# Attention stage of a gated cross-attention and expert kernel: the next group's front product issued before or after the probability-value products

## The reference

```python
x = x + tanh(g_xattn) * attention(layernorm(x), ctx, ctx, mask, Wq, bq, Wk, bk, Wv, bv)
    # Qh, Kh, Vh = 16 heads of 16; probs = softmax(masked(Qh Kh^T / sqrt(10))); probs @ Vh
x = x + tanh(g_ffn) * experts(layernorm(x), Wg, W1, W2, W3)
    # per expert: top-k tokens; silu(xg W1^T) * (xg W3^T) @ W2^T, weighted, added back
```

## Time and profile before

| | |
|---|---|
| median of 3 runs | 1004.09 us (1002.74 to 1007.72) |
| profiled execution, its own time | 999.87 us |
| its span, first to last instruction | 998.1 us |
| mean granted TensorE clock | 0.913 of full speed |
| busy: PE, PEld | 783.9 us (79%), 615.0 us (62%) |
| busy: DVE, ACT, POOL | 608.9 us (61%), 516.7 us (52%), 401.4 us (40%) |
| 256 score maxima, L684 | 165.0 us, 676 ns each |
| 256 exponentials, L541 | 147.6 us, 587 ns each |
| 2048 values matmuls, L852 | 72.1 us |

### The profile page before, as it was taken

How to read it: one execution, slowest core, us unless ns; L and a number is a source line. 1 busy time by engine, 2 the same in 40 slices (tenths; PEclk the granted TensorE clock), 3 DMA queues, 4 the chain that set the end, 5 groups by cost and what they waited for, 6 DMA issues and landing times. The chain is left out here.

```text
span 998.1 us, 22875 instructions
## 1 busy us (share of the span) xinstructions
PE 783.9 (79%) x7244; PEld 615.0 (62%) x7244; DVE 608.9 (61%) x1501; ACT 516.7 (52%) x1002; POOL 401.4 (40%) x777
## 2 busy tenths in 40 slices
PE   3488888798889888987897721116899999999994
PEld 1366666566666665665666511112798899889884
DVE  1457777677667667766767618879545544644530
ACT  2356576657665666666566711000555665666551
POOL 3344334433443344334432132003355675575434
PEclk9799999999999899989999955555899999999997
DMA  3875558656866585667556235001154365453223
GB/s 116 233 202 129 162 173 237 172 167 178 227 156 180 159 220 148 186 185 184 155 144 159 71 94 186 0 1 44 44 109 119 72 128 113 109 92 47 55 33 42
DMA packets 99261, 130.60 MB, mean 131 GB/s; under 512 B 12896, under 2 KB 62336, under 8 KB 99200
## 3 DMA queue, kind: packets, MB, share of 16 engines
q1 hardware_dynamic: 86912, 112.78, 40.2%
q0 software_dynamic: 12288, 17.05, 10.5%
HBM read 52.34 MB, written 26.49 MB: 79 GB/s over the span
## 5 line engine op out<-in xcount | busy, mean ns | idle before, releaser
L684 DVE TENSOR_REDUCE m_sb<-a_ps 128x4 f32<-128x512 f32 x256 | 165.0, 676 | 17.5 <-PE a_ps L825 16.4
L541 ACT ACTIVATE p_t<-b_ps 128x512 f32<-128x512 f32 x256 | 147.6, 587 | 52.4 <-PE b_ps L838 50.3
L1351 POOL DMA_INDIRECT out<-y,idx_add x64 | 100.1, 1565 | 107.8 <-DVE idx_add L1451 71.6
L825 PE MATMUL a_ps<-k_st,q_st 97*128 97x128 bf16 x1024 | 100.2, 221 | 21.7 <-DMA k_st<-k_part 16.2
L1341 POOL DMA_INDIRECT xg<-rows_scratch,idx x64 | 67.7, 1058 | 103.6 <-issue 89.1
L455 POOL TENSOR_TENSOR q_part<-q_rest,q_part 128x512 bf16<-128x512 f32 x32 | 36.9, 1154 | 179.4 <-ACT q_part L512 179.4
L825 PEld LDWEIGHTS a_ps<-k_st,q_st 97*128 97x128 bf16 x1024 | 73.9, 98 | 55.4 <-issue 48.9
L838 PE MATMUL b_ps<-q_st,k_st 99*128 99x128 bf16 x1024 | 100.2, 221 | 4.7 <-ACT p_t L541 4.7
L1549 PE MATMUL bank<-x_hi,w_hi 128*128 128x512 f32 x256 | 100.7, 393 | 1.5 <-DVE x_lo L1477 1.5
L1549 PE MATMUL bank<-x_hi,w_lo 128*128 128x512 f32 x256 | 99.9, 390 | 0.0
L1549 PE MATMUL bank<-x_lo,w_hi 128*128 128x512 f32 x256 | 99.7, 390 | 0.0
(11 more groups left out here) (193 smaller groups left out, 1728.4 us busy)
## 6 DMA issues: line engine op xcount, KB each, us to landing
q_st<-q_part SPq DMA_DIRECT2D x96, 256.0 KB, 4.7
k_st<-k_part SPq DMA_DIRECT2D x96, 256.0 KB, 4.1
w<-in_w_t SPq DMA_DIRECT2D x24, 512.0 KB, 4.9
rows_scratch<-row SPq DMA_DIRECT2D x16, 528.0 KB, 4.1
x_in<-in_x SPq DMA_DIRECT2D x16, 512.0 KB, 4.9
c_t<-in_ctx_t SPq DMA_DIRECT2D x16, 512.0 KB, 4.9
x_res<-in_x SPq DMA_DIRECT2D x16, 512.0 KB, 3.7
out<-x SPq DMA_DIRECT2D x16, 512.0 KB, 3.3
```

The costliest lines, as they stand in the source:

```text
L541: act.activation(p_t[b.s % 2][:, 4 * q:4 * q + 4, :], b_ps[q % 2][:].rearrange("p (h s) -> p h s", s=P), ACT.Exp, scale=SCALE).then_inc(ex ...
L684: dve.tensor_reduce(m_sb[b.s % 2][:, 4 * q:4 * q + 4], a_ps[q % 2][:].rearrange("p (h s) -> p h s", s=P), AX_X, ALU.max).then_inc(max_done, 1)
L825: mm = pe.matmul(a_ps[q % 2][:, i * P:(i + 1) * P], q_st[g.p][0:A_K, h, tok], k_st[g.p][0:A_K, h, tok], start=True, stop=True)
L1351: pool.indirect_dma_start(out[:, :], bass.IndirectOffsetOnAxis(ap=idx_add[e.p][:, st:st + 1], axis=0), y[st][:], None, compute_op=ALU.add) ...
```

## The change

In quarter 2 of each step the front product of the next group is issued before `values`, `router` and `scores_back` instead of behind them. Quarter 0 does the same as before.

```diff
                     if q == OT_AT:
                         out_back(b)
                     scores_t_(*((b.back(2), q - 1) if q else (b.back(3), 3)))
+                    if q in (0, 2):
+                        front(g.on(1), 2 * b.j + q // 2)
                     if q == 2:
                         for i in range(4):
                             values(b.back(3), i)
...
                         if b.j == 1:
                             scores_back(g.on(-3), b)
-                    if q in (0, 2):
-                        front(g.on(1), 2 * b.j + q // 2)
                     if q == 0:
                         max_t(b)
```

## The result

The changed kernel takes 1012.62 us (median of 18 runs, 1008.32 to 1018.13), the kernel before in the same sittings 1004.68 us (18 runs, 1001.71 to 1008.53). The ratio is 1.0077, with a 95% interval of 1.006 to 1.0093: slower by 7.9 us, where +7.5 us was forecast and 1011.6 us named. The sum came out; its two terms did not, as the traces show: that the total is so near is luck. The profiled executions stand further apart, with spans of 998.1 and 1010.6 us. Of these 12.5 us, 7.3 are there at the last `router_out` (593.19 us after, 585.90 before). The other 5.2 come behind it, where the two programs are the same: that stretch took 412.2 us in the trace of before, 417.4 in that of after and 414.3 to 417.5 in those of the experiments. So the loss that belongs to the change is the one in the attention, and it is near the 7.9 us of the medians.

A forecast was written before the change was run, and what follows sets the result against it. The prediction took a closed chain through GpSimd's `ln1` and `rest_k` to bound the kernel, not TensorE's own work. Delay +4.2 us and clock falls +3.3 us gave +7.5 us on 1004.1, 1011.6 us, range 1003.5 to 1019.

The forecast's parts named there:

- its two terms: The forecast's +4.2 us for a delay in groups 1 to 14 and +3.3 us for more clock falls.
- What bounds the kernel: Claim that a chain through GpSimd, not TensorE's own work, sets the group spacing, 33.36 us in the loop.
- The circle through `split_q`, `ln1`, `rest_k` and `mid_k`: Closed chain from k_st through TensorE, GpSimd and ScalarE back to k_st; its delay reaches the group nearly one for one.
- The forecast's own sign against it: The forecast called itself wrong if groups kept 33.36 us despite the new wait; then the circle would be another.
- The new wait for `rest_q`: Step j = 1: the moved front product u = 3 waits 0.44 us on TensorE for the first half's `rest_q`.
- I take 0.30 us per group: Delay of the third quarter's exp, `mid_q`, `split_q` and `ln1`; over 14 groups +4.2 us.
- 2.0 us idle before L908: TensorE's idle time waiting there for late ScalarE (L561) was to grow from 1.5 to about 2.0 us.
- One or two more clock falls, +3.3 us: Loop groups in which longer TensorE idle time lowers the granted clock, at 2.6 us each, beyond the three before.
- the piece that looked like a small win: Shorter wait before u = 4, 0.83 to about 0.6 us, bringing TensorE about 0.23 us sooner to L908.
- Faster: Rival: u = 3 sooner by 1.18 us speeds `hi_q`, `rest_q`, `mid_q` and GpSimd's start; -16.5 us, 987.6; chance 0.06.
- Nothing: Rival: `rest_q` is in time or slack absorbs the stall; 1004, down to 1001.7 us; chance 0.13.
- clock falls widely: Rival: four to five more clock falls in the loop besides the delay; +16 us, 1020; chance 0.14.

The follow-up runs named there:

- e7: Kernel before, with `ln1` on GpSimd ahead of the two `split_q` in step j = 1 instead of behind them: 973.99 us, ratio 0.9679.
- e4: Kernel before, with 12 extra identity matmuls on TensorE in each group before its wait at L908: 1004.28 us, ratio 0.9982.
- e3: Changed kernel, with 12 extra identity matmuls on TensorE in each group before its wait at L908: 1004.65 us, ratio 0.9988.
- e12: Kernel before, order untouched, with one memset of an unused tile on GpSimd at the start of `ln1`: 1019.09 us, ratio 1.0129.
- e9: Changed kernel, with 6 extra matmuls of 256 columns per group before the wait at L908, in the loop only: 1000.57 us, ratio 0.9948.
- e2: Kernel before, with the front products of steps j = 0, 2 and 3 moved ahead but not that of j = 1: 1005.47 us, ratio 1.0002.
- e6: Kernel before, with 12 extra identity matmuls per group before the wait at L908, in the loop only: 1037.45 us.
- e10: Kernel before, with 6 extra matmuls of 256 columns per group before the wait at L908, in the loop only: 1016.59 us.

## Why the prediction was right in its sum and wrong in its split

*What bounds the kernel: right.* The circle through `split_q`, `ln1`, `rest_k` and `mid_k` held: opening it (e7) gave 3.2%. The forecast's own sign against it, groups that keep 33.36 us despite the new wait, came all the same (33.39). What was wrong is not the circle but how much of the delay reaches `rest_k`.

*The new wait for `rest_q`: right in place, 0.55 us of delay instead of 0.44.* 0.37 us of it are the later start behind the transposed scores (the idle time in the row of L804 is 0.29), 0.18 are seams, where the forecast allowed for some hundredths.

*"I take 0.30 us per group", +4.2 us: wrong, about three times too large.* The spacing grew by 0.03 and 0.18 us in the two groups that can be compared and by 0.10 between e4 and e3, an estimated 1.4 us in all. `mid_q` did slip by 0.38 us, but `rest_k`, at the other end of `ln1`, by less: from the first `rest_q` to this row

```profile
329.14 1.16 POOL L460 TENSOR_TENSOR k_rest<-k_val,k_part 128x512 f32<-128x512 f32 x1 [0.18 <-POOL nm L435]
```

it is 329.14 - 315.48 = 13.66 us, and 392.61 - 379.09 = 13.52 before. Where the other 0.24 us went, two rows of the trace of before show:

```profile
390.32 0.48 DVE L717 SCALAR_TENSOR_TENSOR x<-o_n,gx,x_res 128x256 f32<-128x256 f32 x1
390.39 0.47 POOL L427 TENSOR_TENSOR t<-t,v 128x4 f32<-128x4 f32 x1 [0.18 <-POOL t L426]
```

GpSimd's two-input instruction started inside VectorE's `finish` and took 0.47 us instead of the 0.20 us of its like. In the changed kernel the 0.38 us put another instruction of the chain there, later in that of VectorE, and it got off with 0.22 us:

```profile
326.47 0.49 DVE L717 SCALAR_TENSOR_TENSOR x<-o_n,gx,x_res 128x256 f32<-128x256 f32 x1
...
326.79 0.22 POOL L426 TENSOR_TENSOR t<-y 128x4 f32<-128x4 f32 x1 [0.18 <-POOL y L429]
```

So the two engines got out of each other's way by 0.25 us, and most of the shift was swallowed. It is so in every loop group: before, one instruction of each `ln1` took 0.47 or 0.34 us, in turn, and none did in the changed kernel; from `rest_q` to `rest_k` it is 13.52 or 13.44 us before and 13.66 or 13.62 after. The delay that arrives is 0.14 or 0.18 us. (The Trainium skill, "SBUF — State Buffer", summary of rules, says that of a VectorE and a GpSimd instruction the second one waits fully for the first when VectorE reads two inputs from SBUF and the GpSimd instruction reads SBUF. The rows agree: 390.39 + 0.47 ends within 0.06 us of 390.32 + 0.48.) The step that failed was to carry a delay through a chain of 16 instructions of another engine as if their durations did not depend on when they run. In e12 too 0.52 us put in became 0.35 us of spacing; where the rest of it went was not traced.

*"2.0 us idle before L908": right (1.89 to 1.94), and right in its reason.* It is TensorE's earlier arrival, through the vanished wait before u = 4, that makes most of the growth: counted from the first `rest_q`, u = 4 starts 320.48 - 315.48 = 5.00 us behind it instead of 384.32 - 379.09 = 5.23, and L908 starts 17.12 us behind it instead of 16.99, by these rows, first of after, then of before:

```profile
320.48 1.98 PE L804 MATMUL f_ps<-c_t,wk_sb 128*128 128x512 f32 x4
...
332.60 0.63 PE L908 MATMUL o_ps<-ident,row 128*128 128x128 f32 x4 [1.89 <-ACT row L561]
```
```profile
396.08 0.63 PE L908 MATMUL o_ps<-ident,row 128*128 128x128 f32 x4 [1.52 <-ACT row L561]
```

So of the 0.37 us of growth 0.24 are TensorE's sooner arrival and 0.13 ScalarE's later `normalise2`. The first is the piece that looked like a small win. Before u = 4 I expected 0.6 us of wait to stay, and none did: the stall of 0.55 us in step 1 and the 0.25 us of the sooner `rest_q` fill it.

*"One or two more clock falls, +3.3 us": the mechanism right, the size half of what it was.* There are five more of them. Taken from the loss of 7.9 us, the 1.4 of the delay leave an estimated 6.5 us for them. My price per fall (2.6 us, from one group) was too high, the mean is 6.5 / 5 = 1.3 us, and the number too low. e3, e4 and e9 show that most of the loss is this term: with the idle time filled, 0.4 us of 7.9 is left between the two orders. e12 brings the same falls with no change of TensorE's order.

*The sum is right by luck.* The delay was put some 3 us too high and the clock some 3 us too low, and the two errors cancelled.

*The rivals.* "Faster" by a sooner `mid_q` failed as foreseen: `hi_q` came 0.71 us sooner (318.31 - 315.61 = 2.70 us behind the transposed scores of quarter 2, where it was 382.63 - 379.22 = 3.41), and the exp behind it did not. "Nothing" comes near to the spacing, and "clock falls widely" the number of falls; neither alone gives the time.

*Left open.* Why the move in step j = 1 alone costs more than the whole change by more than its spacing says. Alone, the other moves bring groups 0.1 us closer, which the time of e2 (ratio 1.0002) does not show. And why, with the same idle time of 1.9 us before L908, the clock falls in some groups and not in others, six with j = 1 alone and eight with the whole change and in e12: each number is from one trace.

## What to carry to other kernels

Ask of each wait that a reordering removes where the engine will stand next. Time won ahead of a later, longer wait is only added to it, and on TensorE a longer idle time can cost the clock: here 0.4 us more of it in each group cost most of 8 us. Moving an instruction ahead is safe only if what it needs is ready at the earlier place too (here one `rest_q` was 0.4 us late), and the place worth working on is the head of the circle: two lines that let GpSimd compute its scales first gave 32 us, and with them the order of TensorE made no difference that could be measured.

## What was not expected of the hardware

The same 24 extra matmuls per turn of the loop brought no stop in e4 and made e6 33 us slower than it, where the written-out groups around the loop had fewer instructions; TensorE stood for 8.4 us or more at each of the four jumps back and the instruction queue moved 69 packets instead of 35. With 12 extra matmuls per turn one order of the rest (e9, 33 packets) was free of it and the other (e10, 51 packets) was not, at two of the four jumps. The size of the loop alone does not decide, the same size stood in both; where the loop lies in the program may, and that was not tried.

Four-element instructions on GpSimd went from 0.20 to 0.47 us when they met a VectorE instruction with two inputs in SBUF, which is enough to swallow 0.24 us of a delay of 0.38.
